# Cross attention on one core: maxima spread over thirteen key blocks, VectorE's work laid out in order of time, row-sum additions split by head pair

## The reference, cut to what matters

```python
scores = jnp.einsum('bhqd,bhkd->bhqk', q, k) / np.sqrt(DK).astype(np.float32)
scores = jnp.where(mask == 0, jnp.float32(-1000000000.0), scores)
attn = jax.nn.softmax(scores, axis=-1)
out = jnp.einsum('bhqk,bhkd->bhqd', attn, v)
```

## Time and profile before

| | us |
|---|---|
| median of 3 runs | 4222.03 (4221.62 to 4222.70) |
| the profiled execution, its own time | 4216.29 |
| span of the profile | 4214.5 |
| PE busy | 3869.5 (92%) |
| PEld busy | 2533.4 (60%) |
| DVE busy | 2418.4 (57%) |
| POOL busy | 1487.8 (35%) |
| ACT busy | 1427.4 (34%) |

### The profile page before, as it was taken

How to read it: one execution, slowest core, us unless ns; L and a number is a source line. 1 busy time by engine, 2 the same in 40 slices (tenths; PEclk the granted TensorE clock), 3 DMA queues, 4 the chain that set the end, 5 groups by cost and what they waited for, 6 DMA issues and landing times. The chain is left out here.

```text
span 4214.5 us, 63711 instructions
## 1 busy us (share of the span) xinstructions
PE 3869.5 (92%) x19000; PEld 2533.4 (60%) x19161; DVE 2418.4 (57%) x6242; ACT 1427.4 (34%) x1749; POOL 1487.8 (35%) x804
## 2 busy tenths in 40 slices
PE   4999999979968699999999999999996899986997
PEld 3888888868856344444444444444442687764885
DVE  5444444434446577888878787878883434323235
ACT  2222122222212154554545454544443221112332
POOL 1000000000000366667776666667774223221023
PEclk7999999989979699999999999999997899997999
DMA  3100100145534522122222222222202233226488
GB/s 130 36 31 30 37 30 30 33 154 189 181 131 158 115 43 45 36 45 43 52 53 52 53 52 53 52 53 50 52 6 71 102 108 138 100 93 231 164 295 271
DMA packets 223094, 379.48 MB, mean 90 GB/s; under 512 B 16984, under 2 KB 101496, under 8 KB 222844
## 3 DMA queue, kind: packets, MB, share of 16 engines
q1 hardware_dynamic: 198972, 314.45, 25.8%
q0 software_dynamic: 12640, 41.43, 2.7%
q10 hardware_dynamic: 11232, 20.45, 1.3%
HBM read 228.66 MB, written 147.61 MB: 89 GB/s over the span
## 5 line engine op out<-in xcount | busy, mean ns | idle before, releaser
L1384 DVE CUSTOM_DVE_ANT_0 xa_unread<-xa_mx_ps,mask_q 128x402 bf16<-128x402 f32 x2048 | 1065.4, 574 | 368.4 <-PE xa_mx_ps L1249 198.7
L1351 ACT ACTIVATE xa_prob<-xa_scores 128x1024 f32<-128x1024 f32 (+1 forms) x832 | 835.7, 1024 | 859.2 <-PE xa_scores L1267 756.5
L1229 POOL TENSOR_TENSOR xa_sums<-xa_sums,xa_prob 128x1024 f32<-128x1024 f32 x448 | 1056.6, 2378 | 39.0 <-POOL xa_sums L1229 29.4
L1249 PE MATMUL xa_mx_ps<-xa_kp,xa_qp 96*128 96x402 f32 x2048 | 876.0, 472 | 37.6 <-DMA xa_vg<-values 34.7
L1264 PE MATMUL xa_scores<-xa_qp,xa_kp 97*128 97x512 f32 (+1 forms) x1664 | 707.2, 461 | 14.8 <-issue 7.6
L1249 PEld LDWEIGHTS xa_mx_ps<-xa_kp,xa_qp 96*128 96x128 f32 x2048 | 383.4, 198 | 354.3 <-DVE xa_maxima L1384 286.4
L1267 PE MATMUL xa_scores<-mask_t,ident_b 128*128 128x512 bf16 (+1 forms) x1504 | 588.6, 391 | 0.0
L1276 PE MATMUL xa_o_ps<-xa_prob,xa_vg 128*32 128x512 f32 (+1 forms) x3328 | 449.0, 605 | 5.6 <-issue 5.6
L1264 PEld LDWEIGHTS xa_scores<-xa_qp,xa_kp 97*128 97x128 f32 (+1 forms) x1664 | 316.3, 190 | 160.0 <-ACT xa_prob L1351 88.9
L1267 PEld LDWEIGHTS xa_scores<-mask_t,ident_b 128*128 128x128 bf16 (+1 forms) x1664 | 163.7, 98 | 360.6 <-issue 343.2
L1229 POOL TENSOR_TENSOR xa_sums<-xa_prob 128x1024 f32<-128x1024 f32 x64 | 151.3, 2385 | 570.8 <-ACT xa_prob L1351 570.8
(11 more groups left out here) (273 smaller groups left out, 6112.0 us busy)
## 6 DMA issues: line engine op xcount, KB each, us to landing
xa_kp<-kT_high SPq DMA_DIRECT2D x32, 800.5 KB
ex_src<-sorted_in SPq DMA_DIRECT2D x78, 256.0 KB, 2.7
sorted_out<-ex_made ACTq DMA_DIRECT2D x78, 256.0 KB, 2.4
xa_qp<-qT_high SPq DMA_DIRECT2D x32, 512.0 KB
xa_kp<-kT_low SPq DMA_DIRECT2D x16, 800.5 KB
cxl_rows<-in_ctx SPq DMA_DIRECT2D x16, 768.0 KB, 5.6
values<-cxl_v SPq DMA_DIRECT2D x48, 256.0 KB
xa_vg<-values SPq DMA_DIRECT2D x16, 768.0 KB
```

The costliest lines, as they stand in the source:

```text
L1229: pool.tensor_tensor(sums[pr][:, :, :], left[pr][:, :, :], right[pr][:, :, :], ALU.add).then_inc(pool_added, 1)
L1249: pe.matmul(mx_ps[slot % 3][:, 0:MKEYS], qp[par][0:MAXROW, j, first:first + P], kp[par][0:MAXROW, j, MFIRST[kb]:MFIRST[kb] + MKEYS], start ...
L1351: act.activation(prob[ring][pr][0:keys, :, :], scores[pr][0:keys, :, :], ACT.Exp, scale=SCALE).then_inc(exped, 1)
L1384: dve.tensor_tensor_reduce(out=unread[slot % 2][:, :], in0=mx_ps[slot % 3][:, 0:MKEYS], in1=mask_q[:, half * QB + qt, MFIRST[kb]:MFIRST[kb ...
```

## The change

It has three parts, all in `cross_attention`. **Maxima:** ten of the 64 slots of a unit are now made two units ahead, in steps 9 to 12 (3, 3, 2, 2), and the other 54 one unit ahead, six in each of steps 0 to 8; the order of the banks and the places of the row of maxima and of the sums follow from `place_of`. Ahead of the loop stand ten more. **VectorE:** its program follows the steps: the reads of a step, then in odd steps one addition, in steps 2, 4, 6 and 8 a quarter (128 x 128) of the reciprocal of the unit before, in step 10 the output product. **Additions:** pair 0 is added by GpSimd for all blocks 1 to 11; pair 1 by VectorE for odd blocks and by GpSimd for even blocks, each waiting for the other; ScalarE waits by pair.

```diff
-    SLOTS_OF = [2, 7, 8, 8, 8, 8, 8, 8, 7] + [0] * (KT - 9)
-    SLOT_OF = [sum(SLOTS_OF[:n]) for n in range(KT + 1)]
-    assert SLOT_OF[KT] == SLOTS
     TURN = 9
-    OWN = {"pool": tuple(range(9)), "dve": (9, 10, 11)}
-    POOL_ADDS, DVE_ADDS = len(OWN["pool"]) - 1, len(OWN["dve"])
+    EARLY_OF = {9: 3, 10: 3, 11: 2, 12: 2}
+    EARLY = sum(EARLY_OF.values())
+    LATE = (SLOTS - EARLY) // TURN
+    assert TURN * LATE + EARLY == SLOTS and (SLOTS + 2) % 3 == 0
+    BEFORE = KT - 1
+    POOL_EVEN, DVE_ODD = (BEFORE - 1) // 2, BEFORE // 2
...
-        peak_ps, sum_ps = mx_ps[0], mx_ps[1]
+        peak_ps, sum_ps = mx_ps[(SLOTS - EARLY) % 3], mx_ps[(SLOTS + 1) % 3]
...
+        def early(kt):
+            first = sum(EARLY_OF[n] for n in range(TURN, kt))
+            return range(first, first + EARLY_OF[kt])
+        def late(kt):
+            return range(EARLY + LATE * kt, EARLY + LATE * (kt + 1))
+        def place_of(slot):
+            return slot - EARLY if slot >= EARLY else SLOTS - EARLY + 1 + slot
+        def mx_bank(slot):
+            return mx_ps[place_of(slot) % 3]
...
+            if pr == 0:
+                eng.wait_ge(added_0, (BEFORE - 1) * (u + 1) + max(kt, 1) + 1)
+            elif max(kt, 1) % 2:
+                eng.wait_ge(added_odd, DVE_ODD * (u + 1) + (max(kt, 1) + 1) // 2 + 1)
             else:
-                eng.wait_ge(pool_added, PAIRS * (POOL_ADDS * u + max(OWN["pool"].index(kt), 1)) + 1 + PAIRS * POOL_ADDS)
+                eng.wait_ge(added_even, POOL_EVEN * (u + 1) + kt // 2 + 1)
...
+                def add(u, kt, at, pr, done):
+                    left = prob[at][pr] if kt == 1 else sums[pr]
+                    pool.wait_ge(exped, PAIRS * (KT * u + kt) + pr + 2 + PAIRS)
+                    pool.tensor_tensor(sums[pr][:, :, :], left[:, :, :], prob[(at + kt) % RING][pr][:, :, :],
+                                       ALU.add).then_inc(done, 1)
                 def unit(u, par, half, at, more):
-                    pool.wait_ge(total_made, u + 2)
-                    add(u, 1, prob[at], prob[(at + 1) % RING])
-                    for n, kt in enumerate(OWN["pool"][2:]):
-                        pool.wait_ge(pool_added, PAIRS * (POOL_ADDS * u + n + 1) + 1 + PAIRS * POOL_ADDS)
-                        add(u, kt, sums, prob[(at + kt) % RING])
-                pool.sem_inc(pool_added, PAIRS * POOL_ADDS + 1)
+                    for kt in range(1, BEFORE):
+                        if kt == 1:
+                            pool.wait_ge(total_made, u + 2)
+                        else:
+                            pool.wait_ge(added_0, (BEFORE - 1) * (u + 1) + kt)
+                        add(u, kt, at, 0, added_0)
+                        if kt % 2 == 0:
+                            pool.wait_ge(added_odd, DVE_ODD * (u + 1) + kt // 2 + 1)
+                            add(u, kt, at, 1, added_even)
...
-                    m = SLOTS * u + slot
-                    pe.wait_ge(mx_read, m + 2)
+                    m, place = SLOTS * u + slot, place_of(slot)
+                    after_other = place < 2 or SLOTS - EARLY < place < SLOTS - EARLY + 3
+                    pe.wait_ge(mx_read, m + (3 if after_other else 2))
+                    if place == 2:
+                        pe.wait_ge(sum_kept, u + 1)
+                    if place == SLOTS - EARLY + 3:
+                        pe.wait_ge(row_kept, u + 2)
...
                 def unit(u, par, half, at, more):
                     nxt = (par if half == 0 else 1 - par, 1 - half)
                     for kt in range(KT):
-                        slots = iter(range(SLOT_OF[kt], SLOT_OF[kt + 1]) if more else ())
+                        if kt < TURN:
+                            slots = [(u + 1, *nxt, slot) for slot in late(kt)] if more else []
+                        else:
+                            slots = [(u + 2, 1 - par, half, slot) for slot in early(kt)] if exists(u + 2) else []
+                        def maximum():
+                            if slots:
+                                mx(*slots.pop(0))
                         def between(place):
-                            if kt and (place >= 0 or place == -1 and SLOTS_OF[kt] > 7):
+                            if place >= 0 and kt != TURN and (kt < TURN or place % 2):
                                 maximum()
-                        def maximum():
-                            for slot in itertools.islice(slots, 1):
-                                mx(u + 1, *nxt, slot)
                         for pr in range(PAIRS):
                             if kt + 1 < KT:
@@ -1312,15 +1347,11 @@
                                 score(u + 1, *nxt, 0, pr, between)
                         if more and kt == TURN:
                             turn_peaks(u + 1)
-                        if SLOTS_OF[kt] > 6:
-                            maximum()
+                            if half == 0 and slots:
+                                pe.wait_ge(loaded, 16 * (LOADS * (u // HALF + 2)))
+                        maximum()
                         weigh(u, par, kt, (at + kt) % RING)
-                        if more and kt == 0:
-                            pe.wait_ge(row_kept, u + 3)
-                            pe.wait_ge(sum_kept, u + 2)
-                            if half == 1:
-                                pe.wait_ge(loaded, 16 * (LOADS * (u // HALF + 2)))
-                        for _ in range(SLOTS_OF[kt]):
+                        while slots:
                             maximum()
                     add_up(u)
...
                 def exp(u, kt, ring):
                     n, keys = KT * u + kt, keys_of(kt)
                     act.wait_ge(weighed, n - RING + 2 + RING)
-                    wait_added(act, u, kt - RING)
                     for pr in range(PAIRS):
+                        wait_added(act, u, kt - RING, pr)
                         act.wait_ge(scored, PAIRS * n + pr + 1)
...
-                def add(u, kt, ring, i, pr):
-                    if i == 0:
-                        dve.wait_ge(pool_added, PAIRS * POOL_ADDS * (u + 1) + 1 + PAIRS * POOL_ADDS)
+                def add(u, kt, at):
+                    if kt == 1:
+                        dve.wait_ge(total_made, u + 2)
                     else:
-                        dve.wait_ge(dve_added, PAIRS * (DVE_ADDS * u + i) + 1 + PAIRS * DVE_ADDS)
-                    dve.wait_ge(exped, PAIRS * (KT * u + kt) + pr + 2 + PAIRS)
-                    mine = sums[pr][:, :, :]
-                    dve.tensor_tensor(mine, mine, prob[ring][pr][:, :, :], ALU.add).then_inc(dve_added, 1)
+                        dve.wait_ge(added_even, POOL_EVEN * (u + 1) + kt // 2 + 1)
+                    dve.wait_ge(exped, PAIRS * (KT * u + kt) + 1 + 2 + PAIRS)
+                    left = prob[at][1] if kt == 1 else sums[1]
+                    dve.tensor_tensor(sums[1][:, :, :], left[:, :, :], prob[(at + kt) % RING][1][:, :, :],
+                                      ALU.add).then_inc(added_odd, 1)
+                def invert(u, half, part):
+                    if part == 0:
+                        dve.wait_ge(sum_kept, u + 3)
+                    here = slice(part * P, (part + 1) * P)
+                    dve.reciprocal(sum_sb[half][:, here], sum_sb[half][:, here]).then_inc(inverted, 1)
                 def finish(u, half):
-                    dve.wait_ge(sum_kept, u + 3)
-                    dve.reciprocal(sum_sb[half][:, :], sum_sb[half][:, :]).then_inc(inverted, 1)
-                    dve.wait_ge(inverted, u + 3)
+                    dve.wait_ge(inverted, QB * (u + 1) + 1)
                     dve.wait_ge(o_kept, u + 3)
                     dve.wait_ge(stored, 16 * (u + 2))
                     dve.tensor_tensor(out[:, :], o_sb[half][:, :], sum_sb[half][:, :], ALU.mult).then_inc(finished, 1)
                 def unit(u, par, half, at, more):
-                    for slot in range(SLOTS) if more else ():
-                        read(u + 1, 1 - half, slot)
-                    if more:
-                        peak(u + 1)
-                    for i, kt in enumerate(OWN["dve"]):
-                        for pr in range(PAIRS):
-                            add(u, kt, (at + kt) % RING, i, pr)
-                    if not (isinstance(u, int) and u == 0):
-                        finish(u - 1, 1 - half)
+                    first = isinstance(u, int) and u == 0
+                    for kt in range(KT):
+                        if kt < TURN:
+                            for slot in late(kt) if more else ():
+                                read(u + 1, 1 - half, slot)
+                        elif exists(u + 2):
+                            for slot in early(kt):
+                                read(u + 2, half, slot)
+                        if more and kt == TURN - 1:
+                            peak(u + 1)
+                        if kt % 2 and kt < BEFORE:
+                            add(u, kt, at)
```

(15 more changed lines are left out.)

25 lines of the change are left out of this document (12 added, 13 removed).

## The result

| | before | after |
|---|---|---|
| median | 4222.36 (4 runs) | 4293.14 (4 runs, 4292.85 to 4295.59) |
| ratio | | 1.0169 [1.0151, 1.0187] |
| the profiled execution, its own time | 4216.29 | 4293.36 |
| span | 4214.5 | 4291.5 |
| PE busy | 3869.5 | 3923.3 |

The account below looks back on a forecast made before the run. TensorE bounds a unit, partly waiting for VectorE to free banks. Units 1 to 29 add 93 us, unit 0 1.4, unit 30 1.5, ahead 2: 98 us together, median 4320 us, range 4262 to 4420.

Parts of the forecast that it names:

- The narrower range, 4290 to 4350: Whole kernel: the forecast's own range, from pauses and the work ahead of the loop; given chance 0.62.
- The stall of today, 2.4 us a unit: Cross attention before the change: TensorE waits for VectorE to free banks, 2.4 us a unit, taken as what can be won.
- 3.05 + 0.17 for each maximum: Unstalled key block: 3.05 us between weighings without maxima, plus 0.17 us per maximum; 4.07 us with six.
- The 13.81 us that the prediction gives to five steps: Unit before the change: time from the weighing of key block 9 to that of block 0, with no maxima.
- Stalls behind additions (0.93) and quarters (0.59): Steps 1 to 7: VectorE's work delays the next reads, TensorE stalls 0.93 or 0.59 us; 5.6 us a unit.
- The loads "cost at nothing": Next head group's keys, wanted one unit earlier, some 42 us after issue: 0 us, from a DMA share of 0.46.
- Rival B, the lock: VectorE's and GpSimd's additions block each other: 4463 us, or 4412 if the reciprocal is held as well; chance 0.15.
- That case of B: VectorE's reciprocal quarters are held during GpSimd's additions, 92 us, 4412 us; two thirds of the 0.15 chance.
- Rival A: Cross attention gets faster: even spreading removes the stall, 31 x 2.4 less and 2 more, 4150 us; chance 0.13.
- Rival C (quarters hide): Steps 2, 4 and 6: reciprocal quarters cost nothing, only additions stall; 1.77 x 29 less, 4269 us; chance 0.07.
- The last unit at 0: Unit 31, without maxima: GpSimd and VectorE make the same 22 additions, costed at 0.
- ahead of the loop and unit 0: Ten more reads ahead of the loop, 2 us (between 0 and 5); unit 0, without reciprocals, 1.4 us.

Follow-up runs that it names:

- The even spread: The change with its maxima places kept, reciprocal quarters ahead of the last reads, and additions as before the change; 4190.09 us, ratio 0.9931.
- The two runs with late loads: Next head group's loads issued three weighings later: in the changed kernel 4257.90 us, ratio 1.0085; in the kernel before, ratio 0.9973.

## Why the prediction was right, point by point

The sign, the range and the mechanism were right: 4293 in 4262 to 4420, 27 us under the forecast of 4320. The sum came closer than its terms deserved, as two errors opposed each other, and that is luck: with the stalls right and the loads still at nothing it would have been about 4269, 7 us above the lower end. The narrower range, 4290 to 4350, was luck as well: its terms (pauses of 0 and 0.2 in seven intervals, 0 to 5 ahead of the loop) give 4306 to 4351, and nothing on record gives 4290.

- *The stall of today, 2.4 us a unit: mis-sized.* The even spread without VectorE's work in the way gives 53.3 us, so 1.4 us of 54.7 can be won. I had built the unstalled unit from 3.05 + 0.17 for each maximum; with six a step takes 4.17 and not 4.07, and eight such intervals are 0.8 of the 1.0 us between the two. (The 13.81 us that the prediction gives to five steps are four intervals; its sum of thirteen is right.)
- *Stalls behind additions (0.93) and quarters (0.59): the mechanism shown, both sizes too high* (0.60 and 0.27), by 0.10 for the unstalled step and 0.23 for the overlap of VectorE's neighbours. I had added durations and pauses of 0.04 to 0.06; the pauses are negative. A unit thus stalls 3.2 us, not 5.6, and the sum is 3.2 - 1.4 = +1.8 instead of +3.2, 52 us instead of 93.
- *The loads "cost at nothing": the step that failed.* I read the DMA share of one unit, and that unit holds no loop return; in the fourth units the same load collides with it. The two runs with late loads show 35 us of it in the change and 12 before, so the term was 23 us, 24 by the table.
- *Rival B, the lock: real, but it decided nothing here.* As forecast GpSimd's addition follows VectorE's in the odd blocks. Where they meet, at the end of a unit, VectorE is held (2.21 for 1.22, 1.68 for 0.69), and nobody waits there. That they never meet, as the prediction had it, is wrong. In the run with additions moved up it did decide, and the one with GpSimd's additions small took the hold away. By the Trainium skill (SBUF — State Buffer, "SBUF: two separate sides") operations of VectorE with two SBUF inputs, or in a 2-port mode, and GpSimd's exclude each other; the trace agrees for additions and product. The quarters have one input and take 0.95 us beside GpSimd's; that fits too, if they run in no 2-port mode, which no run here shows. That case of B, the greater part of its chance, is refuted.
- *Rival A: false for the change, true for its first part.* Its point was that anything behind the sixth read must fit in some 0.3 us; additions and quarters do not. Put elsewhere the spread gains 1.4 us a unit.
- *Rival C (quarters hide) is refuted* by the run that moved them: 23 us.
- *The last unit at 0* gained 1.5 us; *ahead of the loop and unit 0* 3.4 against 3.8.

## What to carry to other kernels

With operations that free a resource on an in-order engine (here the reads of three banks), ask of each other operation on it not how long it is but what stands behind it and by when that is wanted; one place further up, into a pause that the engine has anyway, the same operation can cost nothing, as the quarters did; the additions did not, for there they met GpSimd's. If the two that share the work can also exclude each other, place both together. And look at the length of all passes of a loop, not of one: what happens once in four units is not seen in the stretch that one happens to read.
